# Layer 0 attention: scores in 32-row and values in 32-column pieces of the array, values one slot further behind the transposes, pT double-buffered

## The reference, cut to what matters

```
q = (LN(x) @ Wq + bq)            # 256 -> 16 heads of 16
k, v = ctx @ Wk + bk, ctx @ Wv + bv   # ctx: 77 rows of 192 channels per batch
attn = softmax(clip(q k^T / 4, -1e4, 1e4))   # per head, 77 keys
x = x + tanh(g_xattn[0]) * ((attn v) @ Wo + bo)
```

## Time and profile before

| what | value |
|---|---|
| median of 3 runs | 1470.08 us (1467.53 to 1470.77) |
| the profiled execution's own time | 1470.64 us |
| its span, first to last instruction | 1468.9 us |
| mean granted TensorE clock | 0.921 |
| busy over the span: PE, DVE, ACT, POOL | 86%, 72%, 55%, 40% |
| layer 0 attention | from about 12 to 331 us |

### The profile page before, as it was taken

One profiled execution on the slowest core, in us unless ns is written; L12 is line 12 of the kernel. 1 busy time (PEld: TensorE's weight loads), 2 busy tenths in 40 slices (PEclk: granted clock), 3 DMA queues, 4 the chain that ended last, 5 costly groups with the idle time before them and its releaser, 6 DMA issues. The chain is left out here.

```text
span 1468.9 us, 27990 instructions
## 1 busy us (share of the span) xinstructions
PE 1260.1 (86%) x8531; PEld 943.4 (64%) x8578; DVE 1052.2 (72%) x2148; ACT 801.2 (55%) x2378; POOL 582.4 (40%) x599
## 2 busy tenths in 40 slices
PE   3989998986349999999999979957898888949898
PEld 2878787873137777777777744945666656634466
DVE  3988888866655555555555531648999989948898
ACT  2555454542135564555555522636677666727898
POOL 3666666653152222222232100036877767620000
PEclk9999999997659999999999985979999999978999
DMA  3122222217011111111111141020111111100033
GB/s 107 63 84 87 85 86 86 79 47 233 1 51 41 54 43 51 49 43 54 46 46 54 36 137 42 1 61 29 58 59 52 58 52 50 37 19 1 1 109 121
DMA packets 74070, 88.60 MB, mean 60 GB/s; under 512 B 9677, under 2 KB 64323, under 8 KB 73859
## 3 DMA queue, kind: packets, MB, share of 16 engines
q1 hardware_dynamic: 66529, 68.66, 14.7%
q0 software_dynamic: 6816, 18.62, 4.9%
q10 hardware_dynamic: 642, 0.33, 0.1%
HBM read 60.58 MB, written 27.00 MB: 60 GB/s over the span
## 5 line engine op out<-in xcount | busy, mean ns | idle before, releaser
L1078 ACT ACTIVATE exp_h<-exp_ps_h,exp_b_now 128x256 f32<-128x256 f32 x312 | 128.8, 463 | 180.1 <-PE exp_ps_h L1018 176.1
L1018 PE MATMUL exp_ps_h<-exp_xhi,exp_w_now 128*128 128x256 bf16 x1248 | 215.2, 276 | 5.8 <-DVE exp_xlo L1104 5.8
L1612 ACT ACTIVATE a_z<-a_ps_sc,a_nmx 128x77 f32<-128x77 f32 x512 | 159.2, 367 | 98.8 <-DVE a_nmx L1729 98.8
L1122 DVE TENSOR_TENSOR exp_hlo<-exp_h,exp_hhi 128x512 bf16<-128x512 f32 x156 | 107.9, 691 | 95.2 <-ACT exp_hhi L1082 95.2
L1018 PE MATMUL exp_ps_h<-exp_xlo,exp_w_now 128*128 128x256 bf16 x624 | 172.2, 276 | 0.0
L1030 PE MATMUL exp_ps_y<-moe_w2s,exp_hhi 128*128 x585 | 139.2, 379 | 2.0
L1018 PEld LDWEIGHTS exp_ps_h<-exp_xhi,exp_w_now 128*128 128x128 bf16 x1248 | 123.6, 99 | 22.0 <-issue 4.0
L1612 ACT ACTIVATION_READ_ACCUMULATOR a_z<-a_ps_sc,a_nmx 128x1 f32 x512 | 127.7, 249 | 0.0
L1579 PE MATMUL a_ps_o<-a_v_now,a_phi 128*128 128x256 bf16 (+1 forms) x640 | 119.2, 292 | 7.8 <-DVE a_plo L1718 7.6
L986 POOL COPY exp_at_now<-all_token_of 128x2 int32 (+1 forms) x39 | 17.0, 435 | 254.8 <-PE exp_ps_x L1005 252.4
L992 POOL DMA_INDIRECT exp_xg<-xn,exp_at_now x78 | 92.8, 1189 | 41.3 <-POOL exp_at_now L986 29.4
(11 more groups left out here) (250 smaller groups left out, 3083.5 us busy)
## 6 DMA issues: line engine op xcount, KB each, us to landing
a_stage<-in_L_ffn_W_dram SPq DMA_DIRECT2D x64, 256.0 KB, 3.0
y_slots<-exp_y SPq DMA_DIRECT2D x78, 128.0 KB, 1.8
a_x<-in_x_dram SPq DMA_DIRECT2D x32, 128.0 KB, 2.1
x<-a_xo SPq DMA_DIRECT2D x32, 128.0 KB, 1.7
route_x<-x SPq DMA_DIRECT2D x8, 512.0 KB, 7.7
xn<-route_x SPq DMA_DIRECT2D x8, 512.0 KB, 3.0
a_x<-x SPq DMA_DIRECT2D x32, 128.0 KB, 2.2
x<-a_xob SPq DMA_DIRECT2D x32, 128.0 KB, 1.7
```

The lines of the kernel that those rows point to most:

```text
L1018: mm = pe.matmul(ps_h[:, i, f % 2 * SLOT_T:(f % 2 + 1) * SLOT_T], w1_now[:, v, k, hl, f * P:(f + 1) * P], xx[:, k, :], start=(q == 0), sto ...
L1078: ins = act.activation(h[:, f, :], ps_h[:, i, f % 2 * SLOT_T:(f % 2 + 1) * SLOT_T], ACT.Gelu_apprx_tanh, bias=b1_now[:, v, f:f + 1])
L1122: dve.tensor_tensor(hlo[:, v, 2 * i:2 * i + 2, :].rearrange("p f t -> p (f t)"), h[:, 2 * i:2 * i + 2, :].rearrange("p f t -> p (f t)"), h ...
L1612: ins = act.activation(z[:, u, h * KEYS:(h + 1) * KEYS], ps_sc[:, j, (h - SB[j][0]) * KEYS:(h - SB[j][0] + 1) * KEYS], ACT.Exp, bias=nmx[: ...
```

## The change

Nothing but `attention` is edited.

- Scores: a lane is 32 partitions of qT, that is two heads. `kblk` holds only two heads' keys side by side (154 columns) for each lane, in both groups. Eight matmuls, each with 32 rows and 154 columns, write each lane to its own bank of `ps_sc` (four banks now; `ps_p` shrinks to two). One semaphore step reports all scores of a tile. Maxima and subtraction are one operation each over all 1232 columns; `kblk` is filled by two operations.
- Values: 17 blocks (a chunk and a pair of heads) of 32 columns; each writes 32 partitions of `ps_v`. The order `turns` goes round the four column groups.
- Order: the values of tile T-3, not T-2, are in slot T; `pT` has two buffers; the last two transposes of a tile go to the bank that the first four have left, after the transposes of x. The output projection of T-4 is TensorE's first work in a slot, and the copy to `attnT` ScalarE's last. `SKEW` is 4. The residual is moved ahead of the sums on VectorE.
- Projection of values: 17 blocks x 2 matmuls with 32 moving columns, in slot 2. `wv` is loaded with its columns reordered, by six DMAs. Masks: a whole one is made by two selects and copied in ten pieces.

```diff
-    RING, SKEW = 8, 3
+    blocks = [(c, q) for c in range(RCH) for q in range(ng * LANES) if c * P < (q + 1) * PAIR and (c + 1) * P > q * PAIR]
+    turns = [i for row in itertools.zip_longest(*lanes) for i in row if i is not None]
+    vgroups = [range(0, 16), range(16, len(blocks))]
+    RING, SKEW = 8, 4
@@ tensor, values()
-                            mm = pe.matmul(ps_p[:, j, i * P:(i + 1) * P], ctx_now[0:n, k, at0:at0 + P],
-                                           wv[0:n, k, g * P:(g + 1) * P], start=(k == 0), stop=(k == 1))
+                            mm = pe.matmul(ps_p[:, j, (i - group[0]) * 32:(i - group[0] + 1) * 32], ctx_now[0:n, k, at0:at0 + P],
+                                           wv[0:n, k, q * 32:(q + 1) * 32], start=(k == 0), stop=(k == 1))
@@ tensor, slot
+                if has(T - 4):
+                    pe.wait_ge(s["attn_done"], T - 3)
+                    for g in range(ng):
+                        mm = pe.matmul(ps_o, attnT[:, g, :], wo[:, g, :], start=(g == 0), stop=(g == ng - 1))
+                    mm.then_inc(s["o_done"], 1)
...
+                    wait(pe, s["pT_done"], 3 * (T - 2))
+                    for j in range(2):
+                        turn_p(T - 2, u, j)
                 if has(T):
                     pe.wait_ge(s["qT_done"], T + 1)
+                    wait(pe, s["z_done"], T)
+                    for g in range(ng):
+                        for j in range(LANES):
+                            lane = slice(32 * j, 32 * j + 32)
+                            mm = pe.matmul(ps_sc[:, j, g * PAIR:(g + 1) * PAIR], qT[lane, g, :], kblk[lane, g, :],
+                                           start=True, stop=True)
+                    mm.then_inc(s["scores_done"], 1)
                 if has(T + 1):
                     turn_x(T + 1)
                 if has(T - 2):
+                    pe.wait_ge(s["pT_done"], 3 * (T - 2) + 1)
+                    turn_p(T - 2, u, 2)
+                if has(T - 3):
...
+                    wait(pe, s["xo_done"], T - 3)
+                    for i in turns:
...
+                        mm = pe.matmul(ps_v[32 * j:32 * j + 32, g * P:(g + 1) * P], vblk[0:n, i, :], pT[0:n, 1 - u, c, :],
+                                       start=(c == mine[0]), stop=(c == mine[-1]))
                     mm.then_inc(s["pv_done"], 1)
-                if has(T) and t == 1:
-                    wait(pe, s["pT_done"], 3 * (T - 1))
+                if has(T) and t == 2:
+                    pe.wait_ge(s["pT_done"], 3 * (T - 1))
                     values()
@@ vector
-                for h in range(hpg):
+                for h in range(2):
                     ins = dve.tensor_scalar(kblk[:, :, h * KEYS:(h + 1) * KEYS],
...
+                    dve.wait_ge(s["scores_done"], T + 1)
+                    dve.tensor_reduce(mx[:, :].rearrange("p (i x) -> p i x", i=LANES), scores, AX,
+                                      ALU.max).then_inc(s["max_done"], 1)
...
+                    dve.scalar_tensor_tensor(
+                        out=z[:, u, :].rearrange("p (i x k) -> p i x k", i=LANES, k=KEYS), in0=scores,
```

More of the change, by code:

```diff
@@ L344, in turn_x, with turn_p @@
                 mm.then_inc(s["turned_x"], 1)
+            def turn_p(T, u, j):
+                for c in range(4 * j, min(RCH, 4 * j + 4)):
+                    n = min(P, ROWS - c * P)
+                    mm = pe.transpose(ps_p[0:n, j % 2, c % 4 * P:(c % 4 + 1) * P], z[:, u, c * P:c * P + n], C.ident[:, :])
+                mm.then_inc(s["turned_p"], 1)
             def keys(T, b):
@@ L384, in slot @@
                     pe.wait_ge(s["norm_done"], T - 1)
-                    if t == 2:
+                    if t == 3:
                         pe.wait_ge(s["v_done"], NVG * (b + 1))
[L387 to L398, removed]
+                    wait(pe, s["pT_done"], 3 * (T - 2))
+                    for j in range(2):
+                        turn_p(T - 2, u, j)
                 if has(T):
                     pe.wait_ge(s["qT_done"], T + 1)
[L401 to L408, removed]
+                    wait(pe, s["z_done"], T)
[5 more added lines that the diff above has]
+                    mm.then_inc(s["scores_done"], 1)
                 if has(T + 1):
@@ L411, in slot @@
                 if has(T - 2):
[L412 to L423, removed]
+                    pe.wait_ge(s["pT_done"], 3 * (T - 2) + 1)
+                    turn_p(T - 2, u, 2)
+                if has(T - 3):
+                    if not has(T - 2):
+                        pe.wait_ge(s["pT_done"], 3 * (T - 2))
+                    wait(pe, s["xo_done"], T - 3)
+                    for i in turns:
+                        c, q = blocks[i]
+                        j, g = q // ng, q % ng
+                        mine = [cc for cc, qq in blocks if qq == q]
+                        n = min(P, ROWS - c * P)
+                        mm = pe.matmul(ps_v[32 * j:32 * j + 32, g * P:(g + 1) * P], vblk[0:n, i, :], pT[0:n, 1 - u, c, :],
+                                       start=(c == mine[0]), stop=(c == mine[-1]))
                     mm.then_inc(s["pv_done"], 1)
-                if has(T) and t == 1:
-                    wait(pe, s["pT_done"], 3 * (T - 1))
+                if has(T) and t == 2:
+                    pe.wait_ge(s["pT_done"], 3 * (T - 1))
                     values()
@@ L495, in slot @@
                     turned(T + 1)
+                if has(T - 2):
+                    last = ROWS - (RCH - 1) * P
+                    act.wait_ge(s["turned_p"], 3 * (T - 2) + 3)
+                    act.activation(pT[:, u, RCH - 2, :], ps_p[:, 0, 0:P], ACT.Copy)
+                    act.activation(pT[0:last, u, RCH - 1, :], ps_p[0:last, 0, P:2 * P], ACT.Copy).then_inc(s["pT_done"], 1)
+                if has(T - 3):
+                    act.wait_ge(s["pv_done"], T - 2)
+                    wait(act, s["o_done"], T - 3)
+                    act.activation(attnT[:, :, :].rearrange("p g t -> p (g t)"), ps_v, ACT.Copy).then_inc(s["attn_done"], 1)
                 if t == 4 and has(T + TPB):
@@ L567, in slot @@
                     ln_mean(T + 2, u)
-                if has(T - 2) and t == 2:
-                    if isinstance(T, int) and T == 2:
+                if has(T - 3) and t == 3:
+                    if isinstance(T, int) and T == 3:
                         dve.wait_ge(s["mask_step"], MASKS)
-                    block_values(T - 2, b)
-                if has(T - 1):
-                    sums(T - 1, (t - 1) % 2)
+                    block_values(T - 3, b)
                 if has(T - SKEW):
```

128 lines of the change are left out of this document (64 added, 64 removed).

## The result

| | before | after |
|---|---|---|
| median us (range, runs) | 1468.8 (1465.3 to 1470.8, 4) | 1486.2 (1481.9 to 1488.3, 4) |
| profiled execution, span | 1470.6, 1468.9 | 1484.3, 1482.5 |
| mean granted TensorE clock | 0.921 | 0.903 |

The ratio is 1.0116, 95% interval 1.0088 to 1.0145: the change makes the kernel 1.2% slower, where 1458 us was forecast with a range of 1447 to 1482 (chance of slower: 0.24).

What follows compares the result with a forecast made beforehand. VectorE was taken to close the steady slot's loop, TensorE close behind. Steady slots -7, batch changes -14, projections +8 and +0, start -3, end +3 gave -13 us on 1470.6, so 1458, range 1447 to 1482.

Steps and rivals of the forecast that it cites:

- Projection of the values: TensorE, slots projecting a batch's values: 68 weight loads take 7.55 us, +2.7 three times, +8; the fourth, at the start, 0.
- Rival C: TensorE's clock: were only the four projections cold, 68 loads take twice as long, +30, 1488 us; chance 0.10.
- What bounds the kernel now: Steady slot of layer 0 attention: VectorE closes the loop with one 0.23 us gap, TensorE close to the bound.
- Residual into the gap: VectorE, steady slot: the residual moves ahead of the sums into the idle gap, 0.17 us saved.
- Scores on TensorE: Steady slot: 16 score records take 1.18 us, with only a lane's second record beside the next lane's first.
- Values: TensorE, steady slot: 34 value records of 32 columns take 2.2 us, against 2.45 for 22 records now.
- Signs of being wrong: Scores over 1.5 us, values over 2.7 us, or the granted clock in steady slots leaving 1.00.
- the changes of batch: Intervals where the batch changes: two masked copies to kblk for eight, no clock fall, 8.6 us each, -14 in sum.
- the start: Up to the first exponential: kblk copies -1.8, mask's reduction +0.3, cold scores of 3.75 us halved, -3 in sum.
- the merged operations of VectorE: Steady slot: three maxima become one of 1.45 us against 1.56, three subtractions one of 1.45 against 1.57.
- the stall for attnT: TensorE, steady slot: the output matmul waits 0.65 us for ScalarE's copy, costing nothing while TensorE keeps 0.5 us in hand.
- The end: End of the attention: the last but one tile's values, copy, output and residual come before the last values, +3 us.

Runs made afterwards that it cites:

- e2: Changed kernel, the values' projection keeping its 68 records but each moving its 32 columns up to four times: 1460.2 us, ratio 0.9934.
- e8: Changed kernel with one projection matmul per chunk, columns repeated up to 128, maxima in PSUM and e7's GpSimd order: 1423.6 us, 47 us under the kernel before.
- e10: Changed kernel with one projection matmul per chunk and columns repeated up to 128, residual put back behind the sums: 1445.6 us, ratio 0.9847.
- e9: Changed kernel with the small score and value matmuls issued lane by lane, not round the four lanes: 1486.3 us (one run).
- e13: Changed kernel with all eight score matmuls of a tile on the first 32 partitions, same amount of work: 1527.4 us (one run).
- e7: Changed kernel, one projection matmul per chunk, columns repeated up to 128, GpSimd's second subtraction done for the previous tile before the normalisation: 1442.4 us, ratio 0.9803.
- e11: Kernel before the change with e7's GpSimd order alone: 1461.0 us, ratio 0.9937.
- e1: Changed kernel with one values' projection matmul per chunk of keys, 40 records in place of 68: 1460.4 us, ratio 0.9927.
- e4: e1 with the clip of the maxima as a scalar_tensor_tensor against a constant tile: 1459.8 us, ratio 0.9919.

## Why the prediction was wrong, point by point

- *Projection of the values*, "68 x 0.111 = 7.55 us": the failed step that decided the sign. The projection took 11.87 us. The count and the pace of loads were right (e2: 0.113 us); the clock was not, it fell to 1.2 GHz within the projection, and +30.7 us came for +8. The fourth projection, at the start, was put at +0, and its interval grew from 10.29 to 20.85. Rival C named the cause, at +30 and 1488, with a chance of 0.10. That the time fell close to 1488 is in part luck: the projections were 22.7 us over the forecast, not 30, and the steady slots added 9.5 that C did not have. I held against C that steady slots kept 1.00; but those moved 128 to 462 columns to a load (the keys' loads 77), so they said nothing on 32, and after the change steady slots did not keep 1.00 either.
- *What bounds the kernel now*, "So VectorE closes the loop": wrong. VectorE's busy share included waits for GpSimd, 0.33 us in the clip and 0.42 in the clamp, and the loop closes through GpSimd. -7 us were forecast, +2.5 measured; with the waits shortened (e8) the slot is 7.24. The row that showed it, 0.50 us for 16 elements, was in the trace and I did not read GpSimd beside it. This error stays even without the clock's: e2, which kept the clock, ended at 1460.2, and that this is near 1458 is no support for the forecast, since its slots are 8.35 us and not 7.94.
- *Residual into the gap*: "0.17 saved"; it cost 0.12 (e10).
- *Scores on TensorE*, "I take 1.18": 0.64. The assumption that only the second record of a lane lies beside the next was wrong (e9, e13). *Values*, "I take 2.2": 1.12 at full clock. Both errors were on the safe side and hidden. TensorE's reserve was over 2 us a slot, not 0.5, so the interval with a projection at full clock is 12.1 (e2) and not the 14.35 worked out.
- *Signs of being wrong*: of the three named, one came true, the granted clock left 1.00 in steady slots. The other two did not: at full clock the scores took 0.81 us and the values 1.29.
- Right: the changes of batch (8.93 to 8.99 against 8.6, -13.5 against -14), the start (-2.2 against -3), the merged operations of VectorE (1.43 and 1.44 us), the stall for attnT (0.47 us on TensorE, off the path). The end was +0.6, not +3.

## What to carry to other kernels

Before a sum is made on a busy engine, look for operations of it that are far longer than their size (16 elements in 0.5 us), and compare their ends with those of GpSimd's operations: the true chain may run through that engine. When a matmul is cut into small pieces, count the weight loads that stay full and the columns that move for each; a stage of loads with 32 moving columns fell to half clock, and moving the same columns four times made it faster. Tiling TensorE gave 3.4 times on the scores and nothing to a steady slot while GpSimd's chain set it (8.35 us against 8.24). With GpSimd's order changed alone, the small matmuls still gain nothing in a slot (e7 7.92, e11 7.82). With the clip in PSUM as well the slot is 7.24 (e8), while in e11 TensorE is busy for all 7.82. The kernel before with both edits was not run, so how much of the 47 us is the tiling's stays open.

## What the runs showed of the hardware

- TensorE busy without a gap fell to 1.2 GHz in 68 records with 32 moving columns each (11.87 us); with 128 columns it stayed at 2.4 GHz (7.86 us). With 32 and 64 columns it fell halfway in e1 (5.53 us) and stayed at 2.4 GHz in one projection of e4 (4.65 us).
- 16 fp32 score records on four row lanes take 0.64 us, 0.66 in the other order of issue, on one lane 2.19. Value records on column lanes do depend on the order: 1.12 us round the lanes, 2.51 lane by lane. Why the two differ stays open.
- VectorE operations with SBUF operands (a tensor_scalar, or two inputs) ended behind the GpSimd operation that they met, 0.03 us for 16 elements and 0.65 for 1232; with its input in PSUM the clip took 0.17 us beside a GpSimd operation.
